# First graph convolution: messages by one-hot products alone, from a table in two half-precision parts

## Chip, cores and metric

One NeuronCore of one Trainium2 chip runs the whole kernel. The metric is the device time of one execution in microseconds (us), given as the median of several runs. The engines are named as the profile names them: PE (TensorE matmuls) with PEld (its weight loads), DVE (VectorE), ACT (ScalarE), POOL (GpSimd), SP (SyncE, which here only issues DMAs).

## The reference, cut to what matters

6250 nodes with 512 features pass four layers, each with a residual: a two-layer graph convolution (GCN), a feed-forward net with weights quantised to three values, a third convolution, and a switch layer with 16 experts. The change lies in the first convolution of the GCN:

```python
h = x @ W1                                   # 6250 x 8
msg = h[src] * norm[:, None]                 # 100000 edges, sorted by dst
out = segment_sum(msg, dst, num_segments=N) + b1
h = relu(layernorm(out) * gamma + beta)
```

and in the preparation of the feed-forward weights, which the kernel does in the same stretch:

```python
scale = mean(abs(w_group_of_128)) + EPS
wq = clip(round(w / scale), -1, 1) * scale
```

## The kernel before, in words

The kernel is one program of four blocks with a barrier between them. Block A normalises x, multiplies by W1 and counts degrees. Block B does the first convolution and quantises the feed-forward weights. Block C does the second convolution and the feed-forward net. Block D does the third convolution, the routing and the experts.

Nodes lie in 49 tiles of 128 (`NT`), edges in 784 chunks of 128 (`C`), one edge per partition. For each edge, block B has to fetch the 8 values of its source's row (`msg`), and then to sum the messages of each destination tile.

**Fetching.** There are two ways. The last 344 chunks are gathered on POOL, one indirect DMA of 128 rows per chunk from a row table in DRAM (`hid1_rows`; `gather_units`, L129), in chunk order; four chunks at a time are reported to the sums. The first 440 chunks are fetched by products, 4 chunks to a group, `M` = 110 groups. A source number is split into lo (the half of a 256-row block and the lane) and hi (which of 25 blocks). ACT and DVE build one-hot matrices from the lo numbers, broadcast to all partitions by a DMA (ACT: `far` L1150 and `los` part 0 L1156; DVE: `los` part 1 L988). ACT also builds `beside` (L1154), the distance of hi from each of 25 lanes; the other 103 lanes of that tile stay zero. PE multiplies, for each chunk k of a group (`products`):

```python
nc.tensor.matmul(into, beside[:, g % AHEAD, k * P:(k + 1) * P], outside..., start=True, stop=False)   # L1194
for b in range(2):
    for j in range(3):
        last = nc.tensor.matmul(into, los[:, g % AHEAD, b, k * P:(k + 1) * P], parts[:, j, b]..., ...)  # L1197
```

The table `parts` holds all rows in three bf16 parts. The first product puts a very large negative number on every block but the right one, so that a maximum over the blocks on DVE picks the message (`pick`, L994). Four DVE steps then split the picked values into three bf16 parts in `msg` (`split_picked`, L1007 to L1013). Everything runs `AHEAD` = 3 groups ahead, with three PSUM buffers between PE and DVE; SP loads the lo and hi numbers of one group at a time.

**Weights beside it.** An order written out by hand (`piece_at`) places one piece of weight work after every third group: 22 wide pieces (128 x 512 of the gate or up matrix) and then 4 of the down matrix (128 x 1408). DVE takes the scale and rounds in five passes (L946 to L961), PE transposes in f32 (L1206, L1216), ACT and DVE copy out of PSUM (L1136, L968).

**Sums.** When all products are done, some 30 small steps on DVE work out the range of chunks of each tile (L1051 to L1081, also needed by block D). Then tile by tile: DVE subtracts the tile's first node from the destinations (`rels`, L210) and compares to a 128 x 2560 bf16 one-hot (L213), ACT copies 20 chunks of messages (L228), PE multiplies 20 times (L244), DVE adds the three parts (L1088). Two buffers alternate. A tile whose chunks are gathered waits until they have landed. Layernorm over the 8 values follows on DVE, then a DMA and the barrier.

The order on each engine is the order of the program; POOL's queue holds the gathers, SP's the loads.

Of the kernel before, what the change touches and what calls it, by code (L numbers as in the profile page):

```python
# [4 lines left out]
F32 = mybir.dt.float32  # L5
# [11 lines left out]
P = 128  # L17
# [25 lines left out]
M = 110  # L43
MB = 5
MW = 3
MD = 10
AHEAD = 3
LR = 4
LB = 6
# [3 lines left out]
assert 4 * M * P <= E and 4 * M % V == 0 and M % MB == 0 and 4 * MB == U  # L53
# [11 lines left out]
H = 8  # L65
H3 = 3 * H
# [135 lines left out]
def build_units_beside(nc, dve, t, ahead, units_done, room, ranges, firsts, dstT, numbers, rel, pairs, related, ready, used):  # L202
# [3 lines left out]
    with dve.Fori(0, units) as b:  # L206
        n = built(nc, dve, units_done)
        dve.wait_ge(used, room_for(nc, dve, room))
        at = chunk_at(nc, c0, b, 0, U)
        nc.vector.tensor_scalar(rel, dstT[:, at], firsts[:, t:t + 1], None, ALU.subtract).then_inc(related, 1)  # L210
# [9 lines left out]
def stage_units_beside(nc, act, t, ahead, units_done, room, ranges, msg, mstage, staged, used, msg_ready):  # L220

    c0, units = range_loaded(nc, act, ahead)
    act.reg_mov(room, 1)
    with act.Fori(0, units) as b:
        n = built(nc, act, units_done)
        act.wait_ge(used, room_for(nc, act, room))
        act.wait_ge(msg_ready, (c0 + (U + VS - 1)) // VS + b * (U // VS))
        nc.scalar.copy(mstage[:], msg[:, chunk_at(nc, c0, b, 0, U), :]).then_inc(staged, 1)  # L228
        act.reg_mov(units_done, n + 1)
        act.reg_mov(room, n + 2)  # L230
    load_range(act, ahead, ranges, t + 1)


def sum_rows(nc, pe, t, ahead, units_done, ranges, mstage, identb, zerob, acc, pairs, ready, staged, used):

    _, units = range_loaded(nc, pe, ahead)
    nc.tensor.matmul(acc, identb[:], zerob[:, 0:H3], start=True, stop=False)
# [9 lines left out]
    return nc.tensor.matmul(acc, identb[:], zerob[:, 0:H3], start=False, stop=True)  # L247
# [120 lines left out]
def program(nc, x, src, dst, node_vec, W1, b1, gamma, beta, W2, b2, w_gate, w_up, w_down,  # L368
            alpha, Wg, bg, switch_w, switch_b, expert_w, expert_b, out):
    with ExitStack() as whole:  # L370
# [18 lines left out]
        def dram(name, shape, dt):  # L389
# [10 lines left out]
        hid1_rows = dram("hid1_rows", (NT * P, H3), BF16)  # L400
# [21 lines left out]
        firsts = sb(convs, "firsts", [P, NT], F32)  # L422
        degroot = sb(convs, "degroot", [P, NT], F32)
# [5 lines left out]
            "span var std degs degs_std span_ps spanr row_ps ranges lows highs numbers pool hid1 stored ".split())}  # L429
        x_in = [[sem(f"a_x_in{j}_{k}") for k in range(G)] for j in range(2)]  # L430
        with ExitStack() as ctx:
# [32 lines left out]
            packed = sb(ctx, "packed", [P, NT, H3], BF16)  # L464
            hrest = sb(ctx, "hrest", [P, 2, NT * H], F32)
# [6 lines left out]
            number = sb(ctx, "number_a", [P, P, 2], BF16)  # L472
# [11 lines left out]
            def _(sp):  # L484
# [33 lines left out]
                sp.wait_ge(s["hid1"], 1)  # L518
                sp.dma_start(hid1_rows.rearrange("(p t) f -> p t f", t=NT), packed[:]).then_inc(s["stored"], 16)
                sp.wait_ge(s["stored"], 16)  # L520

            @block.gpsimd
            def _(pool):
# [13 lines left out]
                nc.gpsimd.iota(firsts[:], [[P, NT]], base=0, channel_multiplier=0, allow_small_or_imprecise_dtypes=True)  # L537
                nc.gpsimd.memset(own3[:], 0.0)
                nc.gpsimd.memset(dstT[:, C:DX], FAR).then_inc(s["const"], 1)
                nc.gpsimd.iota(number[:], [[1, P], [0, 2]], base=0, channel_multiplier=0,  # L540
                               allow_small_or_imprecise_dtypes=True).then_inc(s["numbers"], 1)

            @block.vector
            def _(dve):
# [30 lines left out]
                def histogram(i, m):  # L575
# [4 lines left out]
                    nc.vector.tensor_tensor(ol[:, n % HB], bc(number[:].unsqueeze(1), (P, HP, P, 2)), bc(lo_pairs, (P, HP, P, 2)),  # L580
                                            ALU.is_equal).then_inc(s["ol"], 1)
                    nc.vector.tensor_tensor(oh[:, n % HB], bc(number[:, 0:NT].unsqueeze(1), (P, HP, NT, 2)), bc(hi_pairs, (P, HP, NT, 2)),
# [97 lines left out]
                dve.wait_ge(s["h_used"], G)  # L680
# [42 lines left out]
            def _(pe):  # L723
# [66 lines left out]
                nc.tensor.matmul(pD[:, 0:NT], identb[:], zeros[:], start=False, stop=True).then_inc(s["hist"], 1)  # L790

# [10 lines left out]
            "numbered lanes ext_in fence small_in wq ps hi lo_done dve msg onehot used agg agg_used var std hid2 stored "  # L802
            "tail picked d_wq d_ps d_hi d_lo d_out evens odds blanked besides prod reduced parts far numbers related staged fetched".split())}
        w_in = [sem(f"b_w_in{j}") for j in range(2)]
        wd_in = sem("b_wd_in")
        lo_in = [sem(f"b_lo_in{j}") for j in range(LB)]
        hi_in = [sem(f"b_hi_in{j}") for j in range(LB)]
        landed = [sem(f"b_landed{h}") for h in range(2)]
        with ExitStack() as ctx:
            msg = sb(ctx, "msg_b", [P, CX, H3], BF16)  # L810
            sc = sb(ctx, "sc", [P, 3, FB], F32)
# [8 lines left out]
            picked = sb(ctx, "picked", [P, 2, U, H], F32)  # L820
            prest = sb(ctx, "prest", [P, U, H], F32)
            sig = sb(ctx, "bsig", [P, 1], F32)
            number = sb(ctx, "number", [1, CN], F32)
            lanes = sb(ctx, "lanes", [P, 4], F32)
            far = sb(ctx, "far", [P, 4 * P], BF16)
            lo8 = sb(ctx, "lo8", [P, LB, 4 * P], BF16)
            hi8 = sb(ctx, "hi8", [HT, LB, 4 * P], BF16)
            los = sb(ctx, "los", [P, AHEAD, 2, 4 * P], BF16)
# [26 lines left out]
            def piece_at(g, back):  # L855
# [4 lines left out]
                if g < MW * 2 * FB:  # L860
                    return ("wide", g // MW) if g % MW == 0 else (None, 0)
# [1796 lines left out]
```

## Time and profile before

| what | us |
|---|---|
| median of 3 runs | 3362.64 |
| lowest, highest run | 3353.38, 3371.6 |
| span of the profiled execution | 5135.2 |
| block A in it | 0 to 191 |
| block B: gathers on POOL | 196.6 to 651.9 |
| block B: products | 196.5 to 971 |
| block B: sums | 985 to 1084 |
| block C: feed-forward, steady part | 2165 to 3372 |
| block D | 3387 to 5135 |

The profiled execution is much longer than the runs that were timed. A row of the trace gives start, duration, engine, line, operation and the tiles; a grouped row gives the count, the busy time and the mean duration, and then the idle time ahead of the group with what ended it. "issue" is idle time in which the engine waited for nothing that the profile shows. The end of a matmul is modelled, so matmuls overlap in the rows; the distance of their starts is their price.

### The profile page before, as it was taken

What the parts mean: (1) busy time and instruction counts of PE and PEld (TensorE: products, weight loads), DVE (VectorE), ACT (ScalarE), POOL (GpSimd) and SP (SyncE); (2) the same over time, 40 slices, a digit from 0 to 9 for tenths busy, and PEclk for the clock granted to TensorE, in tenths of its full rate; (3) what the DMA queues carried; (4) which work ended last, traced back from release to release, by engine and by line L of the source; (5) the groups of instructions that cost most, each with busy time, mean ns of one, the idle gap of its engine ahead of it and who ended that gap; (6) DMA issues with size and microseconds to landing.
All of it is one profiled execution on the core that took longest, in us unless ns stands there. A gap on an engine that the chain in (4) does not pass through costs nothing. (4 is left out here: it accounts for less than half of the span.)

```text
span 5135.2 us, 61590 instructions
## 1 busy us (share of the span) xinstructions
PE 2982.4 (58%) x17153; PEld 2061.9 (40%) x17154; DVE 1973.4 (38%) x3813; ACT 1285.4 (25%) x2086; POOL 2000.5 (39%) x2038
## 2 busy tenths in 40 slices
PE   7511179631111000299989999956667666665789
PEld 7400068620000000177777777732232232322477
DVE  9300079750000000166666566632223223232366
ACT  3200057410000000144444444420011111111344
POOL 0377700037777777300000000035555455554244
PEclk9555589755555555599999999977888788887799
DMA  3101023210000000022333233345555556555465
GB/s 101 39 5 11 4 64 96 61 41 3 3 3 3 3 3 3 6 91 88 107 95 102 88 104 100 100 151 168 168 170 161 163 173 182 170 161 158 134 193 155
DMA packets 241523, 466.48 MB, mean 91 GB/s; under 512 B 77093, under 2 KB 107069, under 8 KB 241235
## 3 DMA queue, kind: packets, MB, share of 16 engines
q0 software_dynamic: 107264, 235.06, 17.4%
q1 hardware_dynamic: 133970, 227.93, 14.2%
q8 instruction: 138, 2.26, 0.2%
q14 instruction: 151, 1.23, 0.1%
HBM read 395.90 MB, written 73.45 MB: 91 GB/s over the span
## 5 line engine op out<-in xcount | busy, mean ns | idle before, releaser
L1971 POOL DMA_INDIRECT rows<-xn_rows,srcT x784 | 744.2, 949 | 665.4 <-DVEq L2441 440.7
L129 POOL DMA_INDIRECT msg_c<-hid_rows,srcT x744 | 770.0, 1035 | 245.0 <-issue 236.5
L2122 PE MATMUL pV<-rows,oh 128*128 x2240 | 645.5, 435 | 331.6 <-issue 262.2
L2122 PEld LDWEIGHTS pV<-rows,oh 128*128 x2240 | 238.7, 107 | 724.1 <-issue 576.2
L1197 PE MATMUL pG<-parts,los 128*128 128x200 bf16 x2640 | 308.6, 258 | 322.7 <-issue 322.7
L1487 PE MATMUL gates<-xT,wgu_hi 128*128 128x384 f32 (+1 forms) x1848 | 472.3, 377 | 39.2 <-ACT gate_sum L1585 20.6
L1954 POOL IOTA bases<- 128x49 f32 x1 | 0.2, 188 | 1269.8 <-POOLq L387 1269.8
L1518 PE MATMUL accs<-wd,hT 128*128 128x512 f32 x1617 | 405.4, 398 | 16.2 <-DVE hT L1733 16.2
L129 POOL DMA_INDIRECT msg_b<-hid_rows,srcT x344 | 345.5, 1004 | 110.2 <-issue 105.6
L1197 PEld LDWEIGHTS pG<-parts,los 128*128 128x128 bf16 x2640 | 240.9, 100 | 356.0 <-issue 354.2
L1487 PEld LDWEIGHTS gates<-xT,wgu_hi 128*128 128x128 f32 x1848 | 336.4, 190 | 105.4 <-issue 60.9
L1518 PEld LDWEIGHTS accs<-wd,hT 128*128 128x128 f32 x1617 | 303.5, 189 | 88.1 <-issue 28.4
L2435 DVE SCALAR_TENSOR_TENSOR oh<-ids,bases,dstT 128x896 f32 x160 | 184.1, 1150 | 401.4 <-issue 375.8
L2423 DVE TENSOR_TENSOR agg<-agg,pV x161 | 110.1, 684 | 547.9 <-PE pV L2122 348.2
L994 DVE TENSOR_REDUCE picked<-pG 128x32 f32<-128x800 f32 x110 | 108.5, 987 | 462.2 <-remote 359.4
L1433 PE MATMUL accs<-parts_c,los_c 128*128 128x200 bf16 x168 | 47.7, 323 | 305.0 <-issue 304.9
L2273 ACT ACTIVATE wg<-agg,invdeg 128x512 f32 (+1 forms) x49 | 35.3, 721 | 701.7 <-DVEq L118 578.6
L2150 PE MATMUL pW<-wgT,aT 128*128 128x512 f32 x392 | 197.4, 651 | 18.8 <-issue 12.6
L2217 PE MATMUL pY<-weT,erT 128*128 128x512 f32 (+1 forms) x768 | 193.7, 401 | 3.2 <-DVE weT L2547 2.2
L1637 DVE TENSOR_REDUCE msg_c<-accs 128x32 f32<-128x800 f32 x7 | 6.9, 991 | 485.2 <-remote 485.2
L1467 PE MATMUL accs<-w2b,aggT 128*128 128x512 f32 x8 | 8.2, 1125 | 290.1 <-issue 162.2
L1346 POOL MEMSET msg_c<- 128x152 f32 x1 | 0.2, 225 | 447.8 <-POOLq L387 447.8
(432 smaller groups left out, 5300.1 us busy)
## 6 DMA issues: line engine op xcount, KB each, us to landing
wd<-wd_rows SPq DMA_DIRECT2D x154, 512.0 KB
we<-in_L_ffn_expert_w SPq DMA_DIRECT2D x16, 1024.0 KB
lo<-lo_rows SPq DMA_DIRECT2D x110, 128.0 KB
x_rows<-xr SPq DMA_DIRECT2D x49, 256.0 KB, 4.0
xn_rows<-pair SPq DMA_DIRECT2D x49, 256.0 KB
rows<-xn_rows,srcT POOLq DMA_INDIRECT x784
res<-x_rows SPq DMA_DIRECT2D x49, 256.0 KB
x_rows<-agg SPq DMA_DIRECT2D x49, 256.0 KB
```

The costliest lines, as they stand in the source:

```text
L129: nc.gpsimd.indirect_dma_start(msg[:, c, :], None, table, bass.IndirectOffsetOnAxis(ap=srcT[:, c:c + 1], axis=0)).then_inc(landed[u % 2], 16)
L994: nc.vector.tensor_reduce(picked[:, g // MB % 2, 4 * (g % MB):4 * (g % MB) + 4, :].rearrange("p (b c) f -> p b (c f)", b=2), pG[g % AHEAD] ...
L1197: last = nc.tensor.matmul(into, los[:, g % AHEAD, b, k * P:(k + 1) * P], parts[:, j, b].rearrange("p f h -> p (f h)"), start=False, stop=( ...
L1433: last = nc.tensor.matmul(into, los[:, g % AHEAD, b, k * P:(k + 1) * P], parts[:, j, b].rearrange("p f h -> p (f h)"), start=False, stop=( ...
L1487: last = nc.tensor.matmul(ps[:, 0:n], w, v, start=(m == 0), stop=(m == len(terms) - 1))
L1518: last = nc.tensor.matmul(acc4[j][:], h, wd[:, slot, w, :], start=(f == 0 and m == 0), stop=(f == FB - 1 and m == 2))
L1971: nc.gpsimd.indirect_dma_start(rows[:, u % RING, c, :], None, xn2_rows, bass.IndirectOffsetOnAxis(ap=srcT[:, u * Q + c:u * Q + c + 1], axi ...
L2122: last = nc.tensor.matmul(pV[:, ds(to, 1), :].rearrange("p a d -> p (a d)"), oh[:, ds(to, 1), c, :].rearrange("p a d -> p (a d)"), rows[:, ...
L2150: nc.tensor.matmul(pW[:], aT[:, k % 2, c, :], wgT[:, c, :], start=(c == 0), stop=False)
L2217: last = nc.tensor.matmul(pY[f % 2][0:n, :], erT[:, f % 2, j, c, 0:n], weT[:, e % 2, k, c, :], start=(j, k, c) == terms[0], stop=(j, k, c) ...
L2423: nc.vector.tensor_tensor(at, at, pV[:, ds((v + 1) % 2, 1), :].rearrange("p a b -> p (a b)"), ALU.add).then_inc(s["added"], 1)
L2435: nc.vector.scalar_tensor_tensor(oh[:, ds(v % 2, 1)].rearrange("p a q n -> p (a q) n"), bc(ids.unsqueeze(1), (P, Q, P)), bases[:, ds(tile, ...
```

## The change

All 784 chunks of the first convolution are fetched by products (`M` = 196 groups); the 344 gathers, the row table in DRAM and its DMA go. The table is kept in two fp16 parts, scaled by a power of two that block A takes from the largest value (`top`, `scale_of`), and filled in block A (`fill_table`), so each chunk has 4 products with the table instead of 6. The `beside` lanes of four groups share one tile, 32 partitions each, and the product with it uses those 32 rows. One-hots are built for two groups at once (1024 wide), in fp16, with three buffers (`LP`). The picked value is split into two fp16 halves, by ACT and DVE, once per four groups. Weights: ACT takes size and sign, DVE compares and multiplies, gate and up at once (11 pieces instead of 22, after every twelfth group), the even blocks are transposed by bf16 matmuls. In the sums the subtraction moves to ACT, messages have 16 columns, and the sums of all tiles stay in PSUM for two reductions at the end. Core of the diff:

```diff
-M = 110
-MB = 5
-MW = 3
-MD = 10
+M = 196
+MB = 4
+MW = 12
+MD = 14
 AHEAD = 3
-LR = 4
-LB = 6
+LP = 3
+HQ = 32
+AT_LEAST = 14
 LC = 6
 OUTSIDE = -2.0 ** 122
 HT = -(-NT // 2)
-assert 4 * M * P <= E and 4 * M % V == 0 and M % MB == 0 and 4 * MB == U
+assert 4 * M == C and M % MB == 0 and MB == 4 and P == 4 * HQ and HT <= HQ
...
-        hid1_rows = dram("hid1_rows", (NT * P, H3), BF16)
...
+        table1 = sb(convs, "table1", [P, 2, 2, H, HT], F16)
+        outside4 = sb(convs, "outside4", [P, H, HT], BF16)
+        lanes4 = sb(convs, "lanes4", [P, 4], F32)
+        scaling = sb(convs, "scaling", [P, 2], F32)
+        number2 = sb(convs, "number2", [P, P, 2], BF16)
...
-                sp.wait_ge(s["hid1"], 1)
-                sp.dma_start(hid1_rows.rearrange("(p t) f -> p t f", t=NT), packed[:]).then_inc(s["stored"], 16)
-                sp.wait_ge(s["stored"], 16)
...
+                own.step(nc.gpsimd.memset(outside4[:], 0.0))
+                for c in range(4):
+                    own.step(nc.gpsimd.affine_select(out=outside4[:], in_=outside4[:], compare_op=ALU.not_equal, fill=OUTSIDE, base=c * HQ,
+                                                     pattern=[[0, H], [1, HT]], channel_multiplier=-1))
...
+                dve.wait_ge(s["h_used"], G)
+                nc.vector.tensor_reduce(top[:, 0:1], h1[:].rearrange("p t f -> p (t f)"), AX, ALU.max, apply_absolute_value=True).then_inc(s["top"], 1)
+                dve.wait_ge(s["lanes"], 1)
+                own.step(nc.vector.tensor_single_scalar(lane[:, 1:2], lane[:, 0:1], HQ - 1, ALU.bitwise_and))
+                own.step(nc.vector.tensor_scalar_mul(lanes4[:, 1:2], lane[:, 1:2], -1.0))
+                dve.wait_ge(s["top_ps"], 1)
+                own.step(nc.vector.tensor_reduce(top[0:1, 1:2], pL[0][0:1, 0:P], AX, ALU.max))
+                scale_of(nc, own, top[0:1, 1:2].bitcast(I32), bits)
+                dve.sem_inc(s["scale"], 1)
...
+                dve.wait_ge(s["scale_ps"], 1)
+                own.step(nc.vector.tensor_copy(scaling[:], pL[1][:, 0:2]))
                 own.step(nc.vector.tensor_tensor(hid[:], h1[:], bc(dinv[:].unsqueeze(2), (P, NT, H)), ALU.mult))
-                split3(nc, own, packed, hid, hrest)
-                dve.sem_inc(s["hid1"], 1)
-                own.step(nc.vector.tensor_copy(own3[:, 0:NT, 0:H3], packed[:]))
+                own.step(nc.vector.tensor_scalar(scaled1[:], hid[:], scaling[:, 0:1], None, ALU.mult))
+                own.step(nc.vector.tensor_copy(packed[:, :, 0:H], scaled1[:]))
+                own.step(nc.vector.tensor_tensor(packed[:, :, H:H2], scaled1[:], packed[:, :, 0:H], ALU.subtract))
+                fill_table(nc, table1, packed)
...
-        nc.vector.tensor_scalar(rel, dstT[:, at], firsts[:, t:t + 1], None, ALU.subtract).then_inc(related, 1)
...
+        nc.scalar.activation(rel, dstT[:, at], ACT.Identity, bias=minus_firsts[:, t:t + 1]).then_inc(related, 1)
...
+            def sums_at(t):
+                return pW[:, t // HT].rearrange("p a b -> p (a b)")[:, t % HT * H2:(t % HT + 1) * H2]
...
+                def low(p):
+                    if p >= LP:
+                        sp.wait_ge(s["far"], p - LP + 1)
+                        sp.wait_ge(s["odds"], p - LP + 1)
+                    sp.dma_start(lo8[:, p % LP, :], lo_rows[p * 8:p * 8 + 8, :].rearrange("c q -> (c q)").partition_broadcast(P)).then_inc(lo_in[p % LP], 16)
+
+                def high(q):
                     if q >= 2:
-                        sp.wait_ge(s["wq"], q - 1)
-                    w = (w_gate, w_up)[q % 2]
-                    sp.dma_start(wraw[:, q % 2, :, :].rearrange("p a b -> p (a b)"), w[q // 2 * P:(q // 2 + 1) * P, :]).then_inc(w_in[q % 2], 16)
+                        sp.wait_ge(s["besides"], q - 1)
+                    for c in range(4):
+                        g = 4 * q + c
+                        sp.dma_start(hi4[c * HQ:(c + 1) * HQ, q % 2, :],
+                                     hi_rows[g * 4:g * 4 + 4, :].rearrange("c q -> (c q)").partition_broadcast(HQ)).then_inc(hi_in[q % 2], 16)
+
...
-                gather_units(nc, pool, hid1_rows, srcT, msg, landed, s["msg"], 4 * M // V)
...
+                def odd(p):
+                    dve.wait_ge(lo_in[p % LP], (p // LP + 1) * 16)
+                    if p >= LP:
+                        dve.wait_ge(s["prod"], 2 * (p - LP) + 2)
+                    nc.vector.tensor_scalar(los[:, p % LP, 1, :], lo8[:, p % LP, :], lanes4[:, 3:4], None, ALU.is_equal).then_inc(s["odds"], 1)
...
+                def lower_half(q):
+                    dve.wait_ge(s["halves"], q + 1)
+                    at = slice(q * 4 * MB, (q + 1) * 4 * MB)
+                    nc.vector.tensor_tensor(msg[:, at, H:H2], picked[:, q % 2], msg[:, at, 0:H], ALU.subtract).then_inc(s["picked"], 1)
...
-                    own.step(nc.vector.tensor_reduce(scale, w, AX, ALU.add, apply_absolute_value=True))
-                    nc.vector.scalar_tensor_tensor(q[0], w, 2.0, bc(scale.unsqueeze(2), full), ALU.mult, ALU.is_gt)
-                    own.step(nc.vector.scalar_tensor_tensor(q[1], w, -2.0, bc(scale.unsqueeze(2), full), ALU.mult, ALU.is_gt))
-                    own.step(nc.vector.tensor_tensor(q[0], q[0], q[1], ALU.subtract))
+                    own.step(nc.vector.tensor_reduce(total, size, AX, ALU.add))
+                    own.step(nc.vector.tensor_tensor(q, size, bc(half.unsqueeze(2), full), ALU.is_gt))
+                    own.step(nc.vector.tensor_tensor(q, q, sign, ALU.mult))
...
-                def reduce(t):
-                    dve.wait_ge(s["agg"], t + 1)
-                    nc.vector.tensor_reduce(agg[:, t, :], pW[:, t % 2, 0, 0:H3].rearrange("p (a f) -> p f a", f=H), AX, ALU.add).then_inc(s["agg_used"], 1)
+                dve.wait_ge(s["agg"], NT)
+                for k in range(2):
+                    n = min(HT, NT - k * HT)
+                    last = nc.vector.tensor_reduce(agg[:, k * HT:k * HT + n, :],
+                                                   pW[:, k].rearrange("p a b -> p (a b)")[:, 0:n * H2].rearrange("p (t a f) -> p t f a", a=2, f=H),
+                                                   AX, ALU.add)
+                own.step(last)
...
+                def sign(f):
+                    act.wait_ge(w_in, (f + 1) * 32)
+                    if f > 0:
+                        act.wait_ge(s["wq"], f)
+                    nc.scalar.activation(wsize[:], wraw[:], ACT.Abs).then_inc(s["signs"], 1)
+                    nc.scalar.activation(wsign[:], wraw[:], ACT.Sign).then_inc(s["signs"], 1)
...
+                def low(p):
+                    act.wait_ge(lo_in[p % LP], (p // LP + 1) * 16)
+                    if p > 0:
+                        act.wait_ge(s["evens"], p)
+                    nc.scalar.activation(far[:], lo8[:, p % LP, :], ACT.Abs, bias=lanes4[:, 0:1]).then_inc(s["far"], 1)
+                    if p >= LP:
+                        act.wait_ge(s["prod"], 2 * (p - LP) + 2)
+                    act.wait_ge(s["far"], p + 1)
+                    nc.scalar.activation(los[:, p % LP, 0, :], far[:], ACT.Relu, bias=lanes4[:, 2:3], scale=-1.0).then_inc(s["evens"], 1)
+
+                def high(q):
+                    if q >= 2:
+                        act.wait_ge(s["prod"], 4 * (q - 1))
+                    act.wait_ge(hi_in[q % 2], (q // 2 + 1) * 64)
+                    nc.scalar.activation(beside[:, q % 2, :], hi4[:, q % 2, :], ACT.Abs, bias=lanes4[:, 1:2]).then_inc(s["besides"], 1)
...
                 def products(g):
-                    pe.wait_ge(s["besides"], g + 1)
-                    pe.wait_ge(s["evens"], g + 1)
-                    pe.wait_ge(s["odds"], g + 1)
+                    pe.wait_ge(s["besides"], g // 4 + 1)
+                    pe.wait_ge(s["evens"], g // 2 + 1)
+                    pe.wait_ge(s["odds"], g // 2 + 1)
                     if g >= AHEAD:
                         pe.wait_ge(s["reduced"], g - AHEAD + 1)
+                    rows = slice(g % 4 * HQ, (g % 4 + 1) * HQ)
                     for k in range(4):
                         into = pG[g % AHEAD][:, k // 2, k % 2 * H * HT:(k % 2 + 1) * H * HT]
-                        nc.tensor.matmul(into, beside[:, g % AHEAD, k * P:(k + 1) * P], outside[:].rearrange("p f h -> p (f h)"), start=True, stop=False)
+                        at = (g % 2 * 4 + k) * P
+                        nc.tensor.matmul(into, beside[rows, g // 4 % 2, k * P:(k + 1) * P], outside4[rows].rearrange("p f h -> p (f h)"), start=True, stop=False)
                         for b in range(2):
-                            for j in range(3):
-                                last = nc.tensor.matmul(into, los[:, g % AHEAD, b, k * P:(k + 1) * P], parts[:, j, b].rearrange("p f h -> p (f h)"),
-                                                        start=False, stop=(b == 1 and j == 2))
+                            for j in range(2):
+                                last = nc.tensor.matmul(into, los[:, g // 2 % LP, b, at:at + P], table1[:, j, b].rearrange("p f h -> p (f h)"),
+                                                        start=False, stop=(b == 1 and j == 1))
                     last.then_inc(s["prod"], 1)
...
                 for t in range(NT):
-                    j = t % 2
-                    pe.wait_ge(s["agg_used"], t + 1)
-                    sum_rows(nc, pe, t, ahead, units_done, ranges, mstages[j], identb, zerob, pW[:, j, 0, 0:H3], pairs[j],
+                    sum_rows(nc, pe, t, ahead, units_done, ranges, mstages[t % 2], identb, zerob, sums_at(t), pairs[t % 2],
                              s["onehot"], s["staged"], s["used"]).then_inc(s["agg"], 1)
```

The quantisation's buffers, the new semaphores, the copies out of PSUM and a fused step or two of the layernorm are left out here.

## Rows read from the trace of the kernel before

**Rows 1.** first line of the page

```profile
span 5135.2 us, 61590 instructions
```

**Rows 2.** windows: stretch and length, busy time of each engine, clock, DMA share, GB/s

```profile
191.00:660.00 469.00, 62.08 (x232) 25.62 (x232) 22.89 (x44) 16.36 (x25) 350.18 (x353) 0.51 0.11 13
660.00:985.00 325.00, 274.29 (x2981) 264.02 (x2981) 269.84 (x565) 215.34 (x341) 0.00 (x0) 0.93 0.30 87
...
2165.00:3372.00 1207.00, 1123.64 (x6219) 915.29 (x6217) 746.59 (x1530) 580.29 (x967) 0.00 (x0) 0.99 0.30 96
```

**Rows 3.** undisturbed products, 700 to 820: window, and two groups of DVE

```profile
700.00:820.00 120.00, 113.87 (x1285) 110.59 (x1283) 116.16 (x267) 92.13 (x147) 0.00 (x0) 1.00 0.32 93
...
L994 DVE TENSOR_REDUCE picked<-pG 128x32 f32<-128x800 f32 x44 | 43.3, 985 | 0.5
L988 DVE TENSOR_SCALAR los<-lo,lanes 128x512 bf16<-128x512 bf16 x45 | 15.4, 343 | 0.0
```

**Rows 4.** gathers of block B: the page's group; timeline of POOL

```profile
L129 POOL DMA_INDIRECT msg_b<-hid_rows,srcT x344 | 345.5, 1004 | 110.2 <-issue 105.6
...
198.01 0.95 POOL L129 DMA_INDIRECT msg_b<-hid_rows,srcT  x1 [0.31 <-issue]
199.27 0.94 POOL L129 DMA_INDIRECT msg_b<-hid_rows,srcT  x1 [0.30 <-issue]
```

**Rows 5.** timeline of POOL and DVE in block C, 1844 to 1848

```profile
1844.88 1.62 POOL L129 DMA_INDIRECT msg_c<-hid_rows,srcT  x1 [0.30 <-issue]
1846.81 0.94 POOL L129 DMA_INDIRECT msg_c<-hid_rows,srcT  x1 [0.30 <-issue]
...
1844.19 1.49 DVE L180 TENSOR_TENSOR onehot<-numbers_c,rel_c 128x2560 bf16<-128x2560 bf16 x1
```

**Rows 6.** the page's group of block D's gathers

```profile
L1971 POOL DMA_INDIRECT rows<-xn_rows,srcT x784 | 744.2, 949 | 665.4 <-DVEq L2441 440.7
```

**Rows 7.** DVE in block B: one group; timeline from the last pick on

```profile
L1018 DVE COPY parts<-own 128x200 bf16<-128x200 bf16 x6 | 4.2, 773 | 2.1 <-PEq L387 2.1
...
969.81 0.99 DVE L994 TENSOR_REDUCE picked<-pG 128x32 f32<-128x800 f32 x1 [1.18 <-PE pG L1197]
...
979.49 0.18 DVE L2607 COPY tr<-tr 1x49 f32<-1x49 f32 x1
...
984.65 0.23 DVE L210 TENSOR_SCALAR rels<-dstT,firsts 128x20 bf16 x1 [1.71 <-issue]
...
1000.91 1.49 DVE L213 TENSOR_TENSOR onehot<-numbers_b,rels 128x2560 bf16<-128x2560 bf16 x1
...
1002.88 1.49 DVE L213 TENSOR_TENSOR onehot_b<-numbers_b,rels 128x2560 bf16<-128x2560 bf16 x1
```

**Rows 8.** timeline of PE, products at the full granted clock

```profile
700.61 0.60 PE L1206 MATMUL pW<-ident,wq 128*128 128x128 f32 x4
701.05 0.25 PE L1194 MATMUL pG<-outside,beside 128*128 128x200 bf16 x1
...
701.65 0.25 PE L1194 MATMUL pG<-outside,beside 128*128 128x200 bf16 x1
```

**Rows 9.** timeline of PE around narrow matmuls, and a window of the first stretch

```profile
3494.99 3.60 PE L2150 MATMUL pW<-wgT,aT 128*128 128x512 f32 x8
3498.52 0.39 PE L2151 MATMUL pW<-bg,tri 3*128 3x512 bf16 x1
3498.84 1.47 PE L2122 MATMUL pV<-rows,oh 128*128 x6
...
3498.00:3499.00 1.00, 1.00 (x4) 0.20 (x3) 0.98 (x1) 0.00 (x0) 0.70 (x2) 1.00 0.73 221
...
2450.27 1.32 PE L1518 MATMUL accs<-wd,hT 128*128 128x512 f32 x5
2451.51 0.23 PE L254 MATMUL pB<-identb,own_rows 128*32 128x128 bf16 x1
```

**Rows 10.** ACT in the products, 700 to 820

```profile
L1150 ACT ACTIVATE far<-lo,lanes 128x512 bf16<-128x512 bf16 x44 | 31.8, 723 | 2.7
```

More of the change, by code:

```diff
@@ L65 @@
 H = 8
+H2 = 2 * H
 H3 = 3 * H
@@ L428, in program @@
             "dve lists_f lists_ps lists_used lo_hi ol oh hist_used hist "
-            "span var std degs degs_std span_ps spanr row_ps ranges lows highs numbers pool hid1 stored ".split())}
+            "span var std degs degs_std span_ps spanr row_ps ranges lows highs numbers pool lanes top top_ps scale scale_ps ".split())}
         x_in = [[sem(f"a_x_in{j}_{k}") for k in range(G)] for j in range(2)]
@@ L801, in program @@
         s = {n: sem("b_" + n) for n in (
-            "numbered lanes ext_in fence small_in wq ps hi lo_done dve msg onehot used agg agg_used var std hid2 stored "
-            "tail picked d_wq d_ps d_hi d_lo d_out evens odds blanked besides prod reduced parts far numbers related staged fetched".split())}
-        w_in = [sem(f"b_w_in{j}") for j in range(2)]
+            "numbered ext_in small_in wq signs ps hi lo_done dve msg onehot used agg var std hid2 stored halves "
+            "tail picked d_wq d_signs d_ps d_hi d_lo d_out evens odds besides prod reduced far related staged fetched pool tables".split())}
+        w_in = sem("b_w_in")
         wd_in = sem("b_wd_in")
-        lo_in = [sem(f"b_lo_in{j}") for j in range(LB)]
-        hi_in = [sem(f"b_hi_in{j}") for j in range(LB)]
-        landed = [sem(f"b_landed{h}") for h in range(2)]
+        lo_in = [sem(f"b_lo_in{j}") for j in range(LP)]
+        hi_in = [sem(f"b_hi_in{j}") for j in range(2)]
         with ExitStack() as ctx:
-            msg = sb(ctx, "msg_b", [P, CX, H3], BF16)
-            sc = sb(ctx, "sc", [P, 3, FB], F32)
+            msg = sb(ctx, "msg_b", [P, CX, H2], F16)
             vec = sb(ctx, "vec", [P, 3, H], F32)
@@ L893, in keep @@
                                      wdT[:, j, :, :].bitcast(F32)).then_inc(s["d_out"], 16)
-                for g in range(LB):
-                    low(g)
+                high(0)
+                for p in range(LP):
+                    low(p)
+                high(1)
                 wide(0)
-                wide(1)
                 down(0)
@@ L1172, in _ @@
                             wide(i)
+                        if kind == "wide" and back == 4 and i + 1 < FB:
+                            sign(i + 1)
+                        if kind == "down" and back == 4 and i + 1 < DK:
+                            down_sign(i + 1)
+                upper_half(M // MB - 1)
                 units_done, room, ahead = (tally(act, n) for n in ("units_done", "room", "ahead"))
@@ L2622, in newton, with scale_of, fill_table @@
     own.step(nc.vector.tensor_mul(r, r, t))
+def scale_of(nc, own, top, bits):
+    e, both = bits[0:1, 0:1], bits[0:1, 2:4]
+    own.step(nc.vector.tensor_single_scalar(e, top, 23, ALU.arith_shift_right))
+    own.step(nc.vector.tensor_single_scalar(e, e, AT_LEAST, ALU.max))
+    nc.vector.tensor_scalar(both[:, 0:1], e, -1, 253 + AT_LEAST, ALU.mult, ALU.add)
+    own.step(nc.vector.tensor_single_scalar(both[:, 1:2], e, 1 - AT_LEAST, ALU.add))
+    own.step(nc.vector.tensor_single_scalar(both, both, 23, ALU.logical_shift_left))
+def fill_table(nc, table, packed):
+    for j in range(2):
+        for k in range(2):
+            n = (NT + 1 - k) // 2
+            last = nc.vector.tensor_copy(table[:, j, k, :, 0:n].rearrange("p f h -> p h f"), packed[:, k:NT:2, j * H:(j + 1) * H])
+    return last
 def split3(nc, own, out3, val, rest):
```

325 lines of the change are left out of this document (154 added, 171 removed).

## The prediction

> **What bounds the kernel now.** I read the span first: 5135.2 us for the profiled execution [rows 1], 1772.6 us more than the 3362.64 us median of the three runs. The windows by stage say where that goes [rows 2]: while the first convolution's gathers run (191 to 660), PE gets 232 matmuls through in 469 us; in the next 325 us, without gathers, 2981. The profiled execution is stretched wherever GpSimd gathers, so the sum is made on stretches without that stall and on gaps inside the gather row, and then set against the median.
>
> Block B, the part that is rewritten, ends at the last of two paths, because its 49 sums need both. One: 440 chunks fetched by products, 110 groups. In the undisturbed stretch 700 to 820 DVE is busy 116.16 of 120 us and PE 113.87, with 44 picks [rows 3], so 120/44 = 2.7 us a group and 110 x 2.7 = 300 us: over at about 500. Two: 344 gathers on GpSimd from 196.6 on [rows 4]. Two neighbours start 1.26 us apart, so from 196.6 they need 344 x 1.26 = 433 us and end at 630; by the row's busy and idle time the period is (345.5 + 110.2)/344 = 1.32, ending at 652. So the **gathers bound B before**, the sums trail them by tiles, and DVE and PE have slack in the last third.
>
> How late do the sums of before end in an ordinary run? Lower bound: 630 plus some 5 us for the last tile, 635. Upper, from below: a one-hot of 1.49 us on DVE beside a gather made that gather 1.62 us, the next one 0.94 [rows 5], 0.68 us less; if the 49 one-hots of the sums and the 110 smaller ones of the products all hit a gather and cost 0.6 on average, that is 159 x 0.6 = 95 us: 635 + 95 = 730. From above: the median less A (191), less C (its steady part is 1207 us [rows 2], plus an estimated 30 to 90 of opening), less D (784 gathers [rows 6] at 1.26 to 1.35, plus an estimated 340 of experts), B has 480 to 605 and its sums end 15 earlier, at 655 to 780, which narrows nothing. I take **690**, a little above the middle of 635 to 730, since the products keep DVE busy through most of the gathers.
>
> The Trainium skill, "SBUF — State Buffer", section Who interferes with whom, says that a DVE operation with two SBUF inputs holds GpSimd off for the whole instruction if GpSimd reads SBUF. The 1.62 us gather agrees with it; were every one-hot to cost a full wait, the sums of before would end nearer 730 and the change would look 40 us better.
>
> **The change, part by part.**
>
> *Removed:* 344 gathers with their 433 to 455 us, the row table's DMA with its wait, and six copies (4.2 us [rows 7]). *Added in block A:* a maximum, two tiny PE operations, a dozen DVE steps near 0.18 us [rows 7], scaling, splitting and four table copies in place of a three-way split; some 7 us more on DVE against 4.2 us of copies and about 4 us of round trip less, an extra of 0 to 4. I take the first product 2.5 us later: 199.
>
> *Products, 196 groups instead of 110.* Seven matmuls of 200 columns (one L1194, six L1197) take 0.60 us (701.05 to 701.65 [rows 8]), so 85.7 ns each. A chunk now has five, not seven: a group costs 20 x 85.7 = 1.71 us, and 196 groups 336 us, plus about 15 us of weight transposes (the four f32 ones of a piece hold PE for 0.44 us [rows 8]; there are 88 + 44 blocks as before).
>
> *The 32-row matmul.* The "beside" product used 128 rows, most of them zeros; now four groups share one tile and each product uses 32 rows. It stands between products of 128 rows, once per chunk, 784 times. The only bf16 matmul of before with so few rows is the bias row L2151 (3 rows), 49 of them, all alike; the granted clock there is 1.00, as in the products [rows 3, 9]. The eight matmuls ahead take 3.60 us with the last one's 0.59 inside, a step of 0.43; the last starts at 3498.00, and L2151 only at 3498.52: 0.09 late. L2151 has 512 columns, 0.22 us at 0.43 ns a column, yet the next matmul starts 0.32 later: 0.10 late. So a narrow matmul between wide ones costs **about 0.20 us** extra. It is not the change of type: f32 transposes between bf16 products (700.61 to 701.05, four at 0.109 [rows 8]) cost nothing extra. A switch to 32 columns shows the same: the last of five L1518 starts at 2451.19, its step is 0.23, and L254 begins at 2451.51, 0.09 late [rows 9]. Per chunk 0.20, per group 0.80, in all 784 x 0.20 = **157 us on PE**, and PE becomes the bound with 1.71 + 0.80 = 2.51 us a group. Bounds: 0 (if the rows of L2151 are no guide for 32 rows at a moving offset) and 0.25; I take 0.20, as row and column switch agree.
>
> The Trainium skill, "TensorEngine Tiling (Array Packing)", Key Properties, says that changing the tiling mode drains TensorE; "TensorE: Matmul & The Clock Gate", Why this matters for your kernels, that a matmul of 32 rows takes the same time as one of 128. By the second alone the group would be 1.71 us and the sum 157 us shorter; L2151's late start and late successor agree with the first.
>
> *DVE and ACT in the fetch.* DVE: 196 picks x 0.985 = 193; 98 wider one-hots at no more than 2 x 0.343, 67; the rest of DVE's time in 700 to 820 is (116.2 - 43.3 - 15.4)/15 = 3.8 us a weight piece [rows 3], so at most 84 for 22 pieces, 32 for the four long ones and 16 for halves: under 395. ACT: 98 pairs x 2 x at most 1.45 (twice 0.723 [rows 10]), 284, 49 x 0.95 = 47 for four groups' lanes and upper half, and some 50 for Abs, Sign and copies: under 385. Both fit below PE's 508 = 336 + 157 + 15. What they cost is coupling: only three PSUM buffers stand between pick and product, and a weight piece of 5 to 8 us on DVE uses up the two groups' room; 0 to 25 us, I take 7. So the fetch lasts **515 us** (495 to 535).
>
> *SP's queue:* one load per pair (256 KB) and four per four groups, where there were two per group: fewer issues, three pairs ahead (15 us), hidden. *GpSimd* has nothing left to do in B.
>
> *Sums.* They begin after the whole fetch now. From the last pick's start to the first tile's one-hot work: 14.8 us (969.81 to 984.65 [rows 7]), 1.5 less for three dropped splits and 1 more for the pick, so 14.5. Then 49 tiles; a period of 1.97 (1000.91 to 1002.88) is 96.5, less about 1.5 since the subtraction moves to ACT and the small reduction goes: per tile DVE's one-hot of 1.49, ACT and PE alternate through two buffers, and what DVE sheds ACT's chain takes over. 95 to 97; nothing hides it now, whereas before it trailed the gathers. LN's tail loses two operations, 0.4 us.
>
> *Sum:* 199 + 515 + 14.5 + 96 = **825**, against 690: +135 us. 3362.64 + 135 - 0.4 = 3497, rounded to **3495 us**, 4% slower. With the bounds, 495 against 730 gives +75 (3437), 535 against 635 gives +210 (3572).
>
> **The rivals.**
>
> *A. On the other side: the gathers of before were held up and the switch costs nothing.* Then the fetch is 351 plus coupling, 365, and the sums end at 675. Before, with one-hots holding each gather, at 730: -55 us, **3308**. It decides from a gather period above (675 - 5 - 196.6)/344 = 1.38 us. For: rows 5. Against: rows 9; with the switch the point is 1.82 us, beyond any mean seen.
>
> *B. No switch cost, and before as estimated:* 675 to 700 against 690, coupling included: **3363**, no change. For: 32 rows are not 3, and their offset moves with the group. Against: the same as A.
>
> *C. One of the two switches is hidden* (the loads are short, or the way back is covered by queued weights): 784 x 0.1, the fetch 440, sums at 750: +60, **3420**. For: a weight load of 0.09 us could go beside a stream. Against: both late starts in rows 9.
>
> That the change doesn't remove the gathers it names can be ruled out from the diff; 744 of the second convolution stay.
>
> **How the numbers follow.** About 0.5%, 17 us, is what a measurement can tell from no change. Forecast 0.68, C 0.08, B 0.11, A 0.13. The forecast and C are slower, 0.76; B is the same, 0.10, its edges going to either side; A with an edge of B is faster, 0.14. The forecast's own range is 3437 to 3572. To leave out no more than 2 in 10 the range goes down to C and the edge of B, 3370, and up to 3565.
>
> **What would show it.** In the profile after: no gather in B; matmuls of the new product line 86 ns apart except around the 32-row one, where two steps are near 0.18 us; PE busiest in the fetch at about 2.5 us a group, DVE and ACT idle on PE; last pick near 715, last tile near 825, tile period 1.9 to 2.0. Wrong: 86 ns steps throughout and DVE or ACT above 95% at 1.8 to 1.9 us a group (A or B); one long step per chunk (C). If the fetch is as I say and the time still falls, the sums of before ended far later than 690.

## The result, and the profile after

The changed kernel takes 3503.9 us (median of 4 runs, 3491.0 to 3509.6), the kernel before 3358.0: a ratio of 1.041, 95% interval 1.039 to 1.044. The forecast was 3495.

The profiled execution after has a span of 3489.2 us and isn't stretched as the one of before was. The first lines are the windows of block B after (stretch and length, busy time of PE, PEld, DVE, ACT and POOL, granted clock, DMA share, GB/s): the fetch, and a hundred microseconds inside it.

```profile
189.00:706.00 517.00, 516.31 (x4037) 308.61 (x4035) 323.53 (x485) 299.80 (x340) 0.00 (x0) 0.98 0.29 87
300.00:400.00 100.00, 100.00 (x796) 59.93 (x794) 62.40 (x97) 62.12 (x71) 0.00 (x0) 1.00 0.26 81
```

PE has no gap. The 0.98 of the whole fetch comes from its start, where the granted clock is 0.50 until 204.7; after that it is full. DVE, 97% busy in [rows 3], and ACT, 77% there, are 62% busy. POOL does nothing. The timeline of PE shows what fills it:

```profile
400.34 0.25 PE L1246 MATMUL pG<-outside,beside 32*128 32x200 bf16 x1
400.53 0.52 PE L1249 MATMUL pG<-table,los 128*128 128x200 f16 x4
400.98 0.25 PE L1246 MATMUL pG<-outside,beside 32*128 32x200 bf16 x1
401.17 0.52 PE L1249 MATMUL pG<-table,los 128*128 128x200 f16 x4
401.62 0.26 PE L1246 MATMUL pG<-outside,beside 32*128 32x200 bf16 x1
```

A chunk takes 0.64 us (400.34 to 400.98) for five matmuls of 86 ns, 0.43 us. From the 32-row product to the next it is 0.19 us instead of 0.086 (400.34 to 400.53). From the first of the four to the next 32-row product it is 0.45 instead of 0.34 (400.53 to 400.98). The weight loads show where PE stands in these steps:

```profile
400.34 0.09 PEld L1246 LDWEIGHTS pG<-outside,beside 32*128 32x128 bf16 x1 [0.16 <-issue]
400.52 0.28 PEld L1249 LDWEIGHTS pG<-table,los 128*128 128x128 f16 x4
```

The load of the 32-row product starts only with its matmul, and so does the first load after it: neither goes ahead under the running matmul. Between products of one form each load starts some 85 ns ahead of its own matmul (single rows of this trace and of experiment 1). Whether the late load is the cost or only goes with it isn't separated here. The two long steps are those of L2151 in [rows 9], now 784 times.

The picks, one per group, give the length of the fetch, and the one-hots that of the sums (per group: count, min/median/max ns, first and last start):

```profile
L1033 DVE TENSOR_REDUCE picked<-pG x196: 980/992/993, 189.7 to 705.4; 128x32 f32<-128x800 f32 x196
...
L213 DVE TENSOR_TENSOR onehot_b<-number,rels x49: 1491/1493/1494, 719.4 to 809.9; 128x2560 f16<-128x2560 bf16 x49
```

The fetch runs from the first product at 185.4 to the end of the last pick at 706.4, 521 us. The sums start 14.0 us after the last pick starts and have a period of (809.9 - 719.4)/48 = 1.89 us. The two one-hots of [rows 7] are 1.97 apart; over all 49 of the old scheme the mean is 2.02 (experiment 4 below).

### The profile page after: what moved, and what is told of

Same layout as the page of the kernel before. It is cut to its first block and busy times, and to the rows that moved or that the text cites. A ratio compares the mean times of both kernels' runs of the same rounds, so it can differ in the third digit from the quotient of the medians.

```text
span 3489.2 us, 63018 instructions
## 1 busy us (share of the span) xinstructions
PE 2981.6 (85%) x17996; PEld 2033.8 (58%) x17997; DVE 2004.4 (57%) x3646; ACT 1367.6 (39%) x2118; POOL 1626.8 (47%) x1698
## 5 line engine op out<-in xcount | busy, mean ns | idle before, releaser
L131 POOL DMA_INDIRECT msg_c<-hid_rows,srcT x744 | 743.8, 1000 | 239.1 <-issue 225.1
L2171 PE MATMUL pV<-rows,oh 128*128 x2240 | 555.1, 395 | 151.6 <-DVE oh L2484 56.6
L1249 PE MATMUL pG<-table,los 128*128 128x200 f16 x3136 | 410.9, 254 | 0.0
L1033 DVE TENSOR_REDUCE picked<-pG 128x32 f32<-128x800 f32 x196 | 193.7, 990 | 167.6 <-PE pG L1249 167.1
L1249 PEld LDWEIGHTS pG<-table,los 128*128 128x128 f16 x3136 | 226.5, 98 | 77.7 <-issue 3.0
L1246 PE MATMUL pG<-outside,beside 32*128 32x200 bf16 x784 | 201.0, 256 | 14.9 <-ACT los L1182 14.8
L1640 ACT ACTIVATE up_sum<-gates,wscale 128x512 f32<-128x512 f32 (+1 forms) x154 | 97.6, 634 | 217.1 <-PE gates L1536 217.0
L1772 DVE SCALAR_TENSOR_TENSOR up_sum<-pU,wscale,up_sum 128x512 f32<-128x512 f32 (+1 forms) x154 | 105.1, 682 | 128.6 <-ACT up_sum L1640 122.6
L1536 PE MATMUL gates<-xT,wgu_lo 128*128 128x512 f32 (+1 forms) x462 | 171.8, 372 | 0.0
L1536 PE MATMUL pU<-xT,wgu_hi 128*128 128x512 f32 (+1 forms) x616 | 164.2, 389 | 8.0 <-DVE up_sum L1772 8.0
```

The lines of the kernel that those rows point to most:

```text
L131: nc.gpsimd.indirect_dma_start(msg[:, c, :], None, table, bass.IndirectOffsetOnAxis(ap=srcT[:, c:c + 1], axis=0)).then_inc(landed[u % 2], 16)
L1033: nc.vector.tensor_reduce(picked[:, q % 2, 4 * (g % MB):4 * (g % MB) + 4, :].rearrange("p (b c) f -> p b (c f)", b=2), pG[g % AHEAD][:, :, ...
L1246: nc.tensor.matmul(into, beside[rows, g // 4 % 2, k * P:(k + 1) * P], outside4[rows].rearrange("p f h -> p (f h)"), start=True, stop=False)
L1249: last = nc.tensor.matmul(into, los[:, g // 2 % LP, b, at:at + P], table1[:, j, b].rearrange("p f h -> p (f h)"), start=False, stop=(b == ...
L1536: last = nc.tensor.matmul(ps[:, 0:n], w, v, start=(m == 0), stop=(m == len(terms) - 1))
L2171: last = nc.tensor.matmul(pV[:, ds(to, 1), :].rearrange("p a d -> p (a d)"), oh[:, ds(to, 1), c, :].rearrange("p a d -> p (a d)"), rows[:, ...
```

## The experiments

The first four ran on one chip beside the kernel before (median 3363.9 there), the last two likewise (3364.1). The changed kernel's 3503.9 is from the first measurement, where the kernel before had 3358.0, so differences to it are good to some 6 us.

**1. The beside product over 128 rows.** The constant tile is kept four times, with zeros outside the 32 rows of the group, so nothing leaves the 128-row form.

```diff
-        outside4 = sb(convs, "outside4", [P, H, HT], BF16)
+        outside4 = sb(convs, "outside4", [P, 4, H, HT], BF16)
...
-                        nc.tensor.matmul(into, beside[rows, g // 4 % 2, k * P:(k + 1) * P], outside4[rows].rearrange("p f h -> p (f h)"), start=True, stop=False)
+                        nc.tensor.matmul(into, beside[:, g // 4 % 2, k * P:(k + 1) * P], outside4[:, g % 4].rearrange("p f h -> p (f h)"), start=True, stop=False)
```

> The changed kernel, with the beside product over all 128 rows again (the constant tile is kept four times, each with zeros outside its own 32 rows), so that no product leaves the 128-row form; nothing else changes. Theory (each passage into and out of the 32-row product costs 0.09 to 0.10 us, 1568 passages, 157 us on the engine that bounds the fetch): all steps of PE are near 86 ns, the fetch falls from 520 to 365 to 390 us, where DVE (343 busy in it) and PE (336 plus 15) are about level, and the time falls by 130 to 155 us to 3350 to 3375. Rival (the fetch is held by its three PSUM buffers or by DVE and ACT, and PE only fills the time): fetch above 480 us, time 3470 to 3505.

Measured: 3377.5 us (3370.5 to 3391.7), 126 us below the changed kernel; against the kernel before 1.0045, interval 1.0022 to 1.0068. The same five matmuls per chunk, with more rows multiplied, take a third less time. Timeline of PE, then the picks:

```profile
440.32 0.25 PE L1245 MATMUL pG<-outside,beside 128*128 128x200 bf16 x1 [0.25 <-DVE picked L1033]
440.41 0.50 PE L1248 MATMUL pG<-table,los 128*128 128x200 f16 x4
440.75 0.25 PE L1245 MATMUL pG<-outside,beside 128*128 128x200 bf16 x1
...
L1033 DVE TENSOR_REDUCE picked<-pG x196: 977/991/993, 204.9 to 590.0; 128x32 f32<-128x800 f32 x196
```

A chunk is 0.43 us (440.32 to 440.75), as five times 86 ns makes it. The fetch, from the first product at 201.6 to 591.0, is 389 us. The passages account for 163 us of PE's time (784 x 0.208, below) but give back only 132 of the fetch, because PE now waits for DVE. What ended its idle time in the fetch stands behind the arrows (busy, mean ns, idle before):

```profile
L1245 PE MATMUL pG<-outside,beside 128*128 128x200 bf16 x781 | 195.0, 250 | 12.1 <-DVE picked L1033 12.1
...
L1258 PE MATMUL pW<-identb,wthree 128*128 128x128 bf16 x44 | 8.2, 222 | 8.8 <-DVE wodd L997 8.8
L1269 PE MATMUL pW<-ident,wdq 128*128 128x128 f32 x44 | 6.3, 278 | 9.5 <-DVE wdq L1012 9.5
```

Some 30 us: 18 wait for the weight pieces on DVE and 12 for a free PSUM buffer. In the changed kernel PE waits 0.1 us in all for the same work: DVE's slack covers it.

**2. Half the passages.** The 32-row products of two chunks stand side by side.

```diff
-                    for k in range(4):
-                        into = pG[g % AHEAD][:, k // 2, k % 2 * H * HT:(k % 2 + 1) * H * HT]
+                    into = [pG[g % AHEAD][:, k // 2, k % 2 * H * HT:(k % 2 + 1) * H * HT] for k in range(4)]
+                    for pair in ((0, 2), (1, 3)):
+                        for k in pair:
+                            nc.tensor.matmul(into[k], beside[rows, ...], outside4[rows]..., start=True, stop=False)
+                        for k in pair:
...
```

> The changed kernel with the order of the matmuls of a group turned: the two 32-row products of chunks 0 and 2 stand side by side, then their eight 128-row products, then chunks 1 and 3; same matmuls, half the passages (784 for 1568). Theory (the cost lies in the passage): 78 us less, 3415 to 3440, and the step between two neighbouring 32-row products is near 86 ns. Rival (a 32-row product is slow in itself, wherever it stands): no change, 3490 to 3510.

Measured: 3436.1 us (3431.2 to 3440.0), 68 less than the changed kernel. With 0, 784 and 1568 passages the three forms give 3377.5, 3436.1 and 3503.9. Timeline of PE:

```profile
440.15 0.34 PE L1246 MATMUL pG<-outside,beside 32*128 32x200 bf16 x2
440.42 0.86 PE L1251 MATMUL pG<-table,los 128*128 128x200 f16 x8
441.21 0.34 PE L1246 MATMUL pG<-outside,beside 32*128 32x200 bf16 x2
```

Two neighbours on the same 32 rows take 0.34 us together, the second starting 96 ns after the first (median of the trace), 10 more than the 86 of the other steps; into the pair it is 182 ns and out of it 177. So the price is the passage, not the 32 rows.

**3. The 32 rows in the kernel before.**

```diff
-                        nc.tensor.matmul(into, beside[:, g % AHEAD, k * P:(k + 1) * P], outside[:]..., start=True, stop=False)
+                        nc.tensor.matmul(into, beside[0:32, g % AHEAD, k * P:(k + 1) * P], outside[0:32]..., start=True, stop=False)
```

> The kernel before with its beside product over 32 rows and nothing else changed (the other rows were zeros). Theory (before, the gathers end last and the products have slack; PE gets 880 passages, 88 us, so a group takes 3.2 us for 2.7 and the fetch by products ends near 560, still ahead of the gathers' 630 to 650): -5 to +15 us, 3355 to 3375. Rival (the products end last before): +55 us, near 3413.

Measured: 3366.8 us (3358.6 to 3375.1), ratio 1.0002, 0.998 to 1.002. PE got 880 passages, some 0.1 us each, and the time didn't move. The steps around the 32-row product are 182 and 187 ns as in the changed kernel, though here its rows are always the first 32; so a moving row offset isn't the cause. The profiled execution of this kernel has a span of 3369.8 us, so it also shows block B of the old scheme undisturbed, which [rows 2] could not:

```profile
L994 DVE TENSOR_REDUCE picked<-pG x110: 971/991/992, 202.3 to 572.0; 128x32 f32<-128x800 f32 x110
...
L129 POOL DMA_INDIRECT msg_b<-hid_rows,srcT x344: 941/947/2046, 197.5 to 682.9; - x172
...
L213 DVE TENSOR_TENSOR onehot<-numbers_b,rels x25: 1491/1493/1493, 587.8 to 684.6; 128x2560 bf16<-128x2560 bf16 x25
```

The products take 3.4 us a group (2.85 in experiment 4, which has no passages) and end at 573; the last gather is issued by 685, and the last one-hot starts at 684.6. Gathers of 0.95 us alone become 1.67 us beside the sums; timelines of POOL and of DVE:

```profile
600.51 1.67 POOL L129 DMA_INDIRECT msg_b<-hid_rows,srcT  x1 [0.30 <-issue]
602.49 1.66 POOL L129 DMA_INDIRECT msg_b<-hid_rows,srcT  x1 [0.30 <-issue]
...
601.84 1.49 DVE L213 TENSOR_TENSOR onehot_b<-numbers_b,rels 128x2560 bf16<-128x2560 bf16 x1
603.83 1.49 DVE L213 TENSOR_TENSOR onehot<-numbers_b,rels 128x2560 bf16<-128x2560 bf16 x1
```

Each one-hot of the sums meets one gather, and each gather ends as the one-hot ends plus some 0.8 us. By the group of all 344 gathers (busy, mean ns, idle before) the period is (376.0 + 111.7)/344 = 1.42 us:

```profile
L129 POOL DMA_INDIRECT msg_b<-hid_rows,srcT x344 | 376.0, 1093 | 111.7 <-issue 106.6 <-DMA msg_b<-hid_rows,srcT 4.9 <-POOL msg_b L933 0.3
```

The Trainium skill, "SBUF — State Buffer", section Who interferes with whom, says that a DVE operation with two SBUF inputs contends with a GpSimd one that reads SBUF; the 1.67 us agree with that.

The last tile waits for the last gathers (timelines of ACT and of DVE; in experiment 4 the last reduction waits 1.22 us):

```profile
687.40 0.59 ACT L228 COPY mstage<-msg_b 128x480 bf16 x1 [4.95 <-POOLq L936]
...
689.39 0.18 DVE L1088 TENSOR_REDUCE agg<-pW 128x8 f32<-128x24 f32 x1 [3.22 <-PE pW L247]
```

So the sums end at 689.4, bound by the gathers, but only just: without that wait their own pace from 588 would have ended them some 2 us earlier. The run shows that the products had this much slack, and hardly more.

**4. Ten more groups by products in the kernel before.**

```diff
-M = 110
+M = 120
```

> The kernel before with 120 groups by products for 110, so 304 gathers for 344. Theory (gathers end last at about 1.3 us each, sums near 680): the gathers end 52 us earlier, the products 27 us later near 535, and the sums, which start after the products and last 97 us, become the end near 633: 30 to 50 us less, 3310 to 3330. Rival (the products end last): 27 us more, near 3385.

Measured: 3332.3 us (3317.9 to 3338.3), ratio 0.988, 0.985 to 0.992: 32 us less, with more work for PE, ACT and DVE. So the gathers did bound block B before. The size is 2 us outside the expected range, and its reason differs: I let the sums start with the end of the products, near 535, and end at 633, without the 15 us of small steps between; in its profile they start at 555 and end at 655, 34 us ahead of experiment 3:

```profile
L994 DVE TENSOR_REDUCE picked<-pG x120: 971/984/992, 203.8 to 539.4; 128x32 f32<-128x800 f32 x120
...
L129 POOL DMA_INDIRECT msg_b<-hid_rows,srcT x304: 940/945/2193, 198.8 to 624.5; - x152
...
L213 DVE TENSOR_TENSOR onehot<-numbers_b,rels x25: 1491/1492/1494, 555.2 to 652.3; 128x2560 bf16<-128x2560 bf16 x25
```

Here the gathers are over at 625.5 and the sums' own start has become the bound.

**5. Both engines fetch, without passages.** The changed kernel with the product of experiment 1 and 132 groups; the other 256 chunks are gathered from a DRAM table of the two half-precision parts.

```diff
-M = 196
+M = 132
-MW = 12
-MD = 14
+MW = 8
+MD = 12
...
+        hid1_rows = dram("hid1_rows", (NT * P, H2), F16)
...
+                sp.wait_ge(s["hid1"], 1)
+                sp.dma_start(hid1_rows.rearrange("(p t) f -> p t f", t=NT), packed[:]).then_inc(s["stored"], 16)
+                sp.wait_ge(s["stored"], 16)
...
+                gather_units(nc, pool, hid1_rows, srcT, msg, landed, s["msg"], 4 * M // V)
```

> The changed kernel with the 128-row beside product (as e1_full_rows) and with 132 groups by products instead of 196: the last 256 chunks are gathered on GpSimd again, from a table of the two half-precision parts in DRAM. Theory (two paths share the fetch; products 132 x 1.75 plus the weights' share, about 280 us from 204, gathers 256 x 1.26 plus 0.73 us for each one-hot of the sums that meets one, ending near 560): sums from 498 to 592, 94 us earlier than the kernel before: 3260 to 3290, faster than both kernels. Rival (gathers beside products cost the products what they save, through DVE and GpSimd holding each other off, as the gathers' mean of 1.09 us in the profile of the kernel before with 32 rows suggests): sums near 650, 3330 to 3350.

Measured: 3281.6 us (3279.0 to 3285.7), ratio to the kernel before 0.977, 0.973 to 0.981: 2.3% faster than the kernel before, 222 us below the changed one.

```profile
L1040 DVE TENSOR_REDUCE picked<-pG x132: 971/980/993, 204.8 to 485.0; 128x32 f32<-128x800 f32 x132
...
L213 DVE TENSOR_TENSOR onehot_b<-number,rels x49: 1491/1492/1495, 499.2 to 589.9; 128x2560 f16<-128x2560 bf16 x49
```

Last pick at 485, sums from 499 to 592, as worked out. The gathers were held up here too, and end at 550:

```profile
L131 POOL DMA_INDIRECT msg_b<-hid_rows,srcT x256: 939/944/2286, 194.6 to 549.2; - x128
```

Their busy and idle time gives a period of (275.5 + 81.0)/256 = 1.39 us, but they are still over 42 us ahead of the end of the sums, which are bound by their own start. So the rival's contention is there, and the end of block B doesn't depend on it.

**6. The same with the 32-row product.**

```diff
-                        nc.tensor.matmul(into, beside[:, g // 4 % 2, k * P:(k + 1) * P], outside4[:, g % 4].rearrange("p f h -> p (f h)"), start=True, stop=False)
+                        nc.tensor.matmul(into, beside[g % 4 * HQ:(g % 4 + 1) * HQ, g // 4 % 2, k * P:(k + 1) * P], outside4[g % 4 * HQ:(g % 4 + 1) * HQ].rearrange("p f h -> p (f h)"), start=True, stop=False)
```

> As e5_full_rows_m132, but with the 32-row beside product of the change. Theory (passages are paid per chunk fetched by products, 528 x 0.2 = 106 us on PE, and PE bounds with 2.51 us a group): fetch 350 us, sums from 569 to 662, about 65 us above e5_full_rows_m132 and 25 us below the kernel before: 3325 to 3350. Rival (with PE less loaded the passages are hidden beside DVE): within 15 us of e5_full_rows_m132.

Measured: 3354.1 us (3344.0 to 3359.5), ratio 0.997, 0.995 to 0.999; 72.5 us above experiment 5 (65 expected, the rival within 15). The time itself is 4 us above the range I gave. In its profile the last pick starts at 559.5, 74.5 us after that of experiment 5, and the sums at 573.5, 4.5 later than forecast; 10 us below the kernel before were left of the 25 expected, and the rest of that difference is not explained.

Together the runs make a square of the two parts of the change:

| | beside over 32 rows | beside over 128 rows |
|---|---|---|
| all 784 chunks by products | 3503.9 (the change) | 3377.5 |
| 528 by products, 256 gathered | 3354.1 | 3281.6 |

The 32-row form costs 126 and 72.5 us, and fetching the last 256 chunks by products too costs 150 and 96.

## Why the prediction was right

**The step that decided** was the price of a 32-row product between products of 128 rows. I took 0.20 us a chunk from L2151 and L254 in [rows 9]. Between starts (medians) the trace after has 182 ns into the 32-row product, 187 out of it and 96 for the step after that, where steps of one form take 85.7: 96, 101 and 10 ns more, 0.208 us a chunk. The forecast group of 2.51 us became 4 x 0.637 = 2.55, and 521/196 = 2.66 with the weight transposes and a slow start. Experiments 1 and 2 show the passages as the cause, and that the cost falls with their number. The Trainium skill's rule that a change of tiling mode drains TensorE ("TensorEngine Tiling (Array Packing)", Key Properties) agrees with both long steps; it gives no price.

**The sum, term by term.** First product: 199 forecast; 185.4 in the profile after, but 200.8 to 201.6 in the four other variants of the changed kernel, against 197.5 and 198.9 in the two of the old one. The added steps of block A cost about what I had put on them; the 15 us are block A's clock (below). Fetch: 515, 521 measured, but not by my terms:

```profile
L1246 PE MATMUL pG<-outside,beside 32*128 32x200 bf16 x780 | 199.6, 256 | 0.1
...
190.00:200.00 10.00, 10.00 (x49) 5.05 (x47) 7.46 (x13) 7.17 (x7) 0.00 (x0) 0.50 0.49 154
```

PE waited 0.1 us, so the 7 us put down for coupling were not spent. The passages took 6 us more than forecast, and the first 18 chunks, at the clock of 0.50, took 1.05 us each instead of 0.64, some 8 us for which the sum had no term. That 515 came so near is in part luck. Last pick to the first one-hot: 14.5, 14.0 measured. Sums: 96, measured 719.4 to 812.8, 93.4, since the period fell to 1.89; which of the changes to the sums did that was not tried. End of the sums: 825, measured 812.8, and 828 with a first product at 201. The errors of the terms partly cancel.

**The end before** I took as 690 between wide bounds; experiment 3, at the same time as the kernel before, has it at 689.4. The undisturbed period of 1.26 us for a gather was right (1.25 in that profile, by the median); with the hold-ups it is 1.42. The 55 us that I put on the undisturbed 635 were about right in total, but not in their parts. Laid over DVE's operations, the gathers of that profile that met a one-hot of the sums took 1.67 us on average (49 of them, 47 over 1.05), those that met nothing 0.947. The 112 that met a smaller one-hot of the products, which I had counted with the others, took 0.958; 79 that met a weight pass with two SBUF inputs, which I had not counted, took 1.11. Together that is some 36 us from the sums, 13 from the weights and next to nothing from the smaller one-hots. So the nearness of 690, too, is in part luck.

**The rivals.** A and B rested on passages that cost nothing. Experiment 1 is that case, made real: 1.0045 of the kernel before, so B's "no change" is what the change would have been with the 128-row product, and A's 3308 is not reached. A's first half, that gathers were held up by one-hots, is true, and their period lies just beyond its point of 1.38 us; but the sums before ended at 689, not 730, and its fetch of 365 us took 389, for PE then waits some 30 us for DVE's weight pieces and picks. C, one passage hidden, is contradicted by both steps being long.

**Where I was short** was on what PE without passages would do: 365 to 390 us were expected for the fetch of experiment 1, it took 389, and the time came out 2 us above my range. The times of experiments 4 and 6 lie 2 and 4 us above theirs.

## What to carry to other kernels

Here 96 rows of zeros cost a matmul nothing, while a 32-row matmul between 128-row ones cost about 0.2 us for the way there and back: keep a stream of matmuls in one form, pad with zeros, or put the odd ones side by side. Before moving work off an engine that bounds, work out what the receiving engine needs with it: of the splits tried, 256 chunks on GpSimd and 528 on PE was the fastest, and giving PE all 784 cost 96 us more even without passages. And when a profile is stretched, take the price of an operation from an undisturbed stretch and its odd neighbours from wherever they occur: one bias row at the other end of the trace held the answer.

## What the runs showed of the hardware that I had not expected

PE's speed in block A isn't the same from one execution to the next. Ten microseconds of it, in the window 150 to 160 of the profile after and then of experiment 3 (columns as above):

```profile
150.00:160.00 10.00, 10.00 (x143) 9.91 (x144) 9.93 (x16) 6.77 (x11) 0.00 (x0) 0.83 0.01 2
```

```profile
150.00:160.00 10.00, 10.00 (x93) 10.00 (x90) 7.10 (x15) 3.89 (x6) 0.00 (x0) 0.50 0.00 0
```

PE is busy throughout in both, and had been without a gap for the 50 us before. In one the granted clock had come back up, in the other it stayed at the lower of its two levels (0.50, 1.2 GHz), with a third fewer matmuls. By the trace's clock records block A after has 30.7 us at the full clock before its last matmul, the six experiments 10.2 to 13.7 each. That puts the first product some 15 us earlier in this profile than in those of the four variants of the changed kernel, and its run is the shortest of the changed kernel's four, 3491.0. So a difference of 15 us between single executions need not have its cause in the part that was changed. What decides when the clock comes back was not tried.

The clock that a window shows must be read with care at the start of a trace. Experiment 1 and experiment 3, 100 to 110:

```profile
100.00:110.00 10.00, 10.00 (x95) 9.94 (x94) 9.71 (x22) 4.11 (x7) 0.00 (x0) 1.00 0.28 81
```

```profile
100.00:110.00 10.00, 10.00 (x95) 10.00 (x94) 9.58 (x26) 3.99 (x7) 0.00 (x0) 0.50 0.30 90
```

Both get 95 matmuls through in a stretch in which PE never rests, the one at a shown 1.00, the other at 0.50. The first is not a measurement: the clock records of experiment 1 begin at 129.4 us, those of experiment 3 at 85.0, and a stretch without a record is shown as 1.00. The distance of the matmuls' starts settles it. The f32 transposes of 128 columns are 213 ns apart in both windows, and 109 ns apart in experiment 3 between 87 and 95 us, where the record says 1.00: so both windows ran at the lower level.
